# A LoRA router in four 32-column groups, copied and transposed back, and a later split of the next input

## The reference, cut to what matters

```python
def _mole(x, W, b, A, Bm, Rw):
    gates = jax.nn.softmax(jnp.einsum('bsd,de->bse', x, Rw), axis=-1)
    base = jnp.einsum('bsd,dh->bsh', x, W) + b
    z = jnp.einsum('bsd,edr->ebsr', x, A)
    zg = z * jnp.transpose(gates, (2, 0, 1))[..., None]
    lora = jnp.einsum('ebsr,erh->bsh', zg, Bm)
    return base + SCALING * lora
h = _mole(x, W1, b1, A1, B1, R1)
h = jax.nn.relu(h)
return _mole(h, W2, b2, A2, B2, R2)
...
h = _layernorm(x, axis=-1) * (1 + cb) + sb
x = x + gb * _L1_ffn_ref(h, ...)
```

## Time and profile before

| | |
|---|---|
| median of 3 runs | 516.0 us (515.77 to 517.62) |
| the profiled execution | 514.19 us, its span 512.3 us |
| busy, share of the span | PE 482.0 us (94%), DVE 349.8 us, ACT 340.1 us, POOL 170.4 us |
| LoRA turns 2 to 6, from one to the next | 10.9 us each |

### The profile page before, as it was taken

How to read it: one execution, slowest core, us unless ns; L and a number is a source line. 1 busy time by engine, 2 the same in 40 slices (tenths; PEclk the granted TensorE clock), 3 DMA queues, 4 the chain that set the end, 5 groups by cost and what they waited for, 6 DMA issues and landing times.

```text
span 512.3 us, 11888 instructions
## 1 busy us (share of the span) xinstructions
PE 482.0 (94%) x4560; PEld 387.1 (76%) x4560; DVE 349.8 (68%) x1009; ACT 340.1 (66%) x648; POOL 170.4 (33%) x244
## 2 busy tenths in 40 slices
PE   8699989999999999998997999999999998999994
PEld 6567877787678777876776777877877687998884
DVE  6986887779686978373685876778767673545433
ACT  4968958775877578965765676766767555555640
POOL 2610540034102201210426347274472815343311
PEclk9869999999999999999999999999999999999998
DMA  8600000000000300000322221312213000001001
GB/s 297 207 0 2 2 0 1 0 3 0 1 1 2 142 1 1 1 1 7 116 80 89 80 75 59 113 49 77 86 47 110 7 3 0 22 22 41 22 22 41
DMA packets 24250, 23.44 MB, mean 46 GB/s; under 512 B 3808, under 2 KB 22944, under 8 KB 24064
## 3 DMA queue, kind: packets, MB, share of 16 engines
q1 hardware_dynamic: 23136, 22.12, 13.9%
q10 hardware_dynamic: 1056, 0.52, 0.4%
HBM read 20.27 MB, written 2.36 MB: 44 GB/s over the span
## 4 chain that ended last, share of the span: by engine, by line
PE 43%; issue 3%; POOL 2%; DVE 1%; ACT 1%; SPq 1%; DMA 1%; POOLq 0%
PE bank L170 6%; PE bank L2098 6%; PE bank L172 5%; PE bank L171 5%; PE bank L2008 5%; PE bank L2059 3%; PE bank L2033 3%; PE bank L2048 3%; PE bank L2021 2%; PE bank L246 2%; PE bank L2075 1%; PE bank L2089 1%; PE bank L2068 1%; SPq L1752 1%; DMA att_prob<-cut_rows 1%
## 5 line engine op out<-in xcount | busy, mean ns | idle before, releaser
L1119 PE MATMUL bank<-ffn_g_hi,w_hi 128*128 128x512 f32 x288 | 116.9, 406 | 0.1
L1120 PE MATMUL bank<-ffn_g_lo,w_hi 128*128 128x512 f32 x288 | 114.0, 396 | 0.0
L654 DVE TENSOR_TENSOR ffn_g_lo<-ffn_full,ffn_g_hi 128x512 fp32r<-128x512 f32 x96 | 67.1, 699 | 27.3 <-ACT ffn_full L902 25.9
L1119 PEld LDWEIGHTS bank<-ffn_g_hi,w_hi 128*128 128x128 f32 x288 | 54.3, 188 | 14.0 <-issue 1.9
L1120 PEld LDWEIGHTS bank<-ffn_g_lo,w_hi 128*128 128x128 f32 x288 | 54.3, 188 | 11.7
L902 ACT ACTIVATE ffn_full<-bank,cols 128x512 f32<-128x512 f32 x64 | 44.2, 696 | 21.5 <-PE bank L1120 16.4
L1665 POOL TENSOR_TENSOR att_vw<-att_v,att_prob 128x128 f32<-128x128 f32 x64 | 25.0, 415 | 83.1 <-DVE att_prob L1477 83.1
L1854 ACT COPY att_qT<-bank 128x512 f32<-128x512 f32 x64 | 37.1, 589 | 12.4 <-PE bank L172 8.4
L1477 DVE TENSOR_TENSOR_SCAN att_prob<-att_prob,bank 128x512 f32<-128x512 f32 x32 | 37.5, 1206 | 6.8 <-DMA att_prob<-cut_rows 6.7
L1488 DVE TENSOR_TENSOR att_prob<-bank,att_prob 128x512 f32<-128x512 f32 x32 | 21.9, 690 | 23.6 <-PE bank L2008 22.6
L2098 PE MATMUL bank<-l,att_qT 128*128 128x155 f32 x256 | 37.4, 298 | 0.2 <-ACT att_qT L1827 0.2
(11 more groups left out here) (233 smaller groups left out, 1148.6 us busy)
## 6 DMA issues: line engine op xcount, KB each, us to landing
att_prob<-cut_rows SPq DMA_DIRECT2D x64, 128.0 KB, 3.0
att_wide<-cum_rows SPq DMA_DIRECT2D x64, 56.0 KB, 2.0
out<-att_vw SPq DMA_DIRECT2D x7, 256.0 KB, 2.3
x<-in_x SPq DMA_DIRECT2D x3, 512.0 KB, 11.7
w_raw<-in_w_all SPq DMA_DIRECT2D x1, 1152.0 KB, 8.5
w_raw<-in_w_all SPq DMA_DIRECT2D x1, 768.0 KB, 9.8
x<-in_x ACTq DMA_DIRECT2D x2, 256.0 KB, 3.4
w_raw<-in_w_all SPq DMA_DIRECT2D x1, 512.0 KB, 5.0
```

Of the source, the lines that this page charges most:

```text
L654: dve.tensor_tensor(lo, full[j % 4][:, :], hi.bitcast(F32), ALU.subtract).then_inc(low, 1)
L1119: pe.matmul(acc, w[0], x[0], start=start, stop=False)
L1120: return pe.matmul(acc, w[0], x[1], start=False, stop=stop)
```

## The change

Turns 1 to 6 compute the first router of the next sequence, so of sequences 2 to 7, in another way. The weight is now `ar1` padded with zeros to 32 columns, and the tokens stream: four matmuls of 128x128, one for each token tile, write four groups of 32 PSUM partitions of one bank (`down_rows`, through the helper that the attention gates use, L267 in both kernels). ACT copies that 128x128 block to SBUF (`keep_rows`), and one TensorE transpose puts the tokens back on the partitions (`down_turn`), in the layout that `route` reads. The transpose stands between the two halves of `layer2`, and `layer2_end` moves behind the second half. `bring_high` moves behind `keep_rows` and `ranks(b - 1, 1)`. The bank table follows: the rows take bank 1, the transposed result bank 0, behind the flip of the next input. The order of `layer2_end` and `layer2(b, 1)` changes in turn 7 too.

```diff
@@ constants and weights
-L_WAR2 = L_AR1 + AR
+L_WAR2 = L_AR1 + GLO
-        r["ar1"] = r["l1"][:, L_AR1:L_AR1 + AR]
+        r["ar1"] = r["l1"][:, L_AR1:L_AR1 + GLO]
@@ lora_uses, turn(b)
+                if more:
+                    uses.append((("rows", b + 1, 0), 1))
                 if back:
                     uses.append((("ranks", b - 1, 1), hid_home[b % 2]))
+                uses += ends(b)
                 if more:
-                    uses.append((("down", b + 1, 0), 1))
-                uses += ends(b)
+                    uses.insert(len(uses) - 1, (("down", b + 1, 0), 0))
@@ ACT
+                def keep_rows(b):
+                    act.wait_ge(ring_mm, full("rows", b, 0))
+                    act.copy(router_rows[b % 2][:, :], bank("rows", b, 0)[:, 0:P]).then_inc(rows_ready, 1)
@@ ACT, the turn
                         relu(b, m)
                         if more and m == 1:
                             bring_full(B + b + 1)
-                        if more and m == 2:
-                            bring_high(B + b + 1)
+                    if more:
+                        keep_rows(b + 1)
                     ranks(b - 1, 1)
                     if more:
+                        bring_high(B + b + 1)
                         exps(b + 1, 0)
@@ TensorE
+                def down_rows(b):
+                    pe.wait_ge(h_ready, B + b - 1)
+                    ps = claim(pe, "rows", b, 0)
+                    group_mm(pe, ps, r["ar1"], hT[b % 2]).then_inc(ring_mm, 1)
+                def down_turn(b):
+                    pe.wait_ge(rows_ready, b - 1)
+                    ps = claim(pe, "down", b, 0)
+                    pe.transpose(ps[:, 0:P], router_rows[b % 2][:, :], r["ident"][:, :]).then_inc(ring_mm, 1)
@@ TensorE, the turn
                     if b == 1:
                         output(LAST)
+                    if more:
+                        down_rows(b + 1)
                     flip_ranks(b - 1, 1)
+                    layer2(b, 0)
                     if more:
-                        down(b + 1)
-                    layer2(b, 0)
+                        down_turn(b + 1)
+                    layer2(b, 1)
                     layer2_end(b - 1)
-                    layer2(b, 1)
                     if more:
                         flip_ranks(b + 1, 0)
```

More of the change, by code:

```diff
@@ L261, in gate_rows, with group_mm @@
     return slice(t * GLO, t * GLO + NH)
-def gate_mm(pe, ps, r, hT):
+def group_mm(pe, ps, w, hT):
     for t in range(T):
-        mm = pe.matmul(ps[t * GLO:(t + 1) * GLO, 0:P], r["wg"][:, :], hT[:, t * P:(t + 1) * P], start=True, stop=True)
+        mm = pe.matmul(ps[t * GLO:(t + 1) * GLO, 0:P], w[:, :], hT[:, t * P:(t + 1) * P], start=True, stop=True)
     return mm
@@ L1213, in run @@
                                     pe.wait_ge(att_h_ready, 1)
-                                    gate_mm(pe, claim(pe, "alpha", 0), r, r["h_full"][0]).then_inc(mm, 1)
+                                    group_mm(pe, claim(pe, "alpha", 0), r["wg"], r["h_full"][0]).then_inc(mm, 1)
                         y(i, 0)
@@ L1325, in attention_lora @@
         lora_mm, hid_ready, scaled, res_ready, stored = sem("lora_mm"), sem("lora_hid_ready"), sem("lora_scaled"), sem("lora_res_ready"), pair_sems("stored")
-        end_ready = sem("lora_end_ready")
+        end_ready, rows_ready = sem("lora_end_ready"), sem("lora_rows_ready")
+        router_rows = [sb(f"lora_rows{s}", [P, P]) for s in slots]
         def step_uses(b):
@@ L1410, in __call__ @@
                         "cross": (outer_ready, 2 * b + k + 1), "y": (added, b + 1),
-                        "down": (zg_ready[0], b + 1), "ranks": (zT_ready[k % 2], b + 1), "hid": (hid_ready, b * KH + k + 1),
+                        "down": (zg_ready[0], b + 1), "rows": (rows_ready, b - 1), "ranks": (zT_ready[k % 2], b + 1), "hid": (hid_ready, b * KH + k + 1),
                         "e": (scaled, 2 * b + k + 1),
@@ L1971, in alpha @@
                     ps = claim(pe, "alpha", b, 0)
-                    gate_mm(pe, ps, r, hT[b % 2]).then_inc(ring_mm, 1)
+                    group_mm(pe, ps, r["wg"], hT[b % 2]).then_inc(ring_mm, 1)
                 def values(b):
@@ L2067, in down @@
                     for t in range(T):
-                        mm = pe.matmul(ps[:, t * 32:t * 32 + AR], hT[b % 2][:, t * P:(t + 1) * P], r["ar1"][:, :], start=True, stop=True)
+                        mm = pe.matmul(ps[:, t * 32:t * 32 + AR], hT[b % 2][:, t * P:(t + 1) * P], r["ar1"][:, 0:AR], start=True, stop=True)
                     mm.then_inc(ring_mm, 1)
+                def down_rows(b):
[6 more added lines that the diff above has]
+                    pe.transpose(ps[:, 0:P], router_rows[b % 2][:, :], r["ident"][:, :]).then_inc(ring_mm, 1)
                 def flip_ranks(b, k):
@@ L2236 @@
         "v_all": v_all, "B12": b12,
-        "l1": np.concatenate([tiles(a["L1_attn_Wo"], 2), A1, a["L1_ffn_R1"], tiles(WAR2, KH), bg], 1),
+        "l1": np.concatenate([tiles(a["L1_attn_Wo"], 2), A1, a["L1_ffn_R1"], np.zeros((D, GLO - AR), np.float32), tiles(WAR2, KH), bg], 1),
         "wg": wg,
```

## The result

The changed kernel takes 519.94 us at the median of 22 runs, the kernel before 517.11 at the median of its 22 taken beside it. The ratio is 1.0057, 95% interval 1.0041 to 1.0072: slower by 2.1 to 3.7 us. Runs of either kernel scatter over some 5 us, and much of that arises before the LoRA turns: in the twelve traces here DVE's addition in turn 1 starts anywhere from 431.4 to 436.2 us. So I compare the stretch that the change touches inside the traces. I measure it from the start of DVE's addition in turn 1 to the start of the last addition of all.

The account below looks back on a forecast made before the run. TensorE bounds turns 2 to 6, a DVE and ACT chain the end. Turn 1 +0.25 to +0.37, turns 2 to 5 0 to +0.48, turn 6 -0.10 to -0.24, end +2.17: near +2.6, so 518.6 us, range 516.9 to 520.3.

Parts of the forecast that it names:

- rival 2: Turns 1 to 5: a further wait, the first router's gating late by 0.3 us; +1.5, 520.1 us; chance 0.13.
- The router's cost on TensorE: Turns 2 to 6: new matmuls 0.46 to 0.56 us plus transpose replace 0.81, saving 0.10 to 0.24 a turn.
- The relay over ACT and POOL: Turns 2 to 5: high piece to ranks copy becomes the bound, turns 10.91 to 11.03 us; 0 to +0.48 in all.
- my zero: The place behind layer 1 on TensorE, 454.59 in the old trace, from which the relay's steps are counted.
- Turn 1: Rows wait for DVE's addition with the ranks' transposes now behind them, so L2088 comes +0.25 to +0.37 us later.
- Turn 6: No normalise in this turn, so TensorE's saving counts: -0.10 to -0.24 us.
- The order behind turn 7: layer2_end behind both halves of layer 2 delays scaling and the gatings behind it on DVE: +2.17 us, the largest term.
- The clock: Last stretch: all that follows scaling was taken to keep its length, with no clock term in the sum.
- The first router's gating: Starts later, behind the new transpose; 0.25 to 0.35 us left before the ranks' transposes, so costed at nothing.
- Rival 1: Relay over ACT and POOL does not bind, TensorE keeps its saving in turns 2 to 6; 517.0 to 517.7 us; chance 0.24.
- Rival 3: route_end(0) hangs on layer 2's second half, not scale(6), and the router saves 0.34 a turn; 514.3 us; chance 0.04.
- Rival 4: New router's column groups run one after another, 0.8 to 0.9 us and not 0.36; 520.6 us; chance 0.03.

Follow-up runs that it names:

- e4: Changed kernel with layer2_end ahead of layer 2's second half in turn 7 and POOL's rescale ahead of its low piece; ratio to the kernel before 0.9963.
- e9: Changed kernel with POOL's rescale ahead of its low piece and layer2_end ahead of layer 2's second half in every turn; ratio to the kernel before 0.9954.
- e3: Changed kernel with POOL's rescale ahead of its low piece, the high piece left as changed; ratio to the kernel before 1.0019.
- e1: Changed kernel with layer2_end ahead of layer 2's second half in turn 7 alone, as before; ratio to the kernel before 1.0022.
- e6: Changed kernel with 24 unused transposes of the identity on TensorE behind the last layer2_end; ratio to the kernel before 1.0062.
- e8: Changed kernel with DVE's scale(6) behind both route_end, TensorE's order untouched; ratio to the kernel before 1.0004.
- e7: Changed kernel with the new router's four matmuls all writing the same 32 partitions, one column group; a single run, 521.36 us.
- e2: Changed kernel with the high piece (bring_high) back behind the third relu, as before; ratio to the kernel before 1.0048.

## Why the prediction was right, point by point

I gave 518.6 us and a range of 516.9 to 520.3, on a median of 516.0. The median of the changed kernel is 519.94; that of the kernel before moved to 517.11 with more runs, so the difference is 2.83, where I had 2.6.

Part of that is luck. In the traces the stretch grew by 3.35, outside my sum of 2.2 to 2.9: the clock's 0.45 was not in it, and the relay cost 0.60 where my bound was 0.48. The profiled execution took 518.69, where I had 516.4 to 517.1. The range held the median because it was wide enough for rival 2, which did not come, and of the 1.34 us between 518.6 and 519.94, 1.11 are the rise of the median before. The interval of the difference, 2.1 to 3.7 us, holds the 2.83, the 3.35 and my 2.6 alike. The mechanism is what the traces bear out, term by term.

**The router's cost on TensorE.** The group was 0.35 us, its lead-in 0.11 (0.34 from the wide matmul ahead, in place of 0.23), and the transposes behind it took 0.48 for 0.45: 0.49 in all, inside my 0.46 to 0.56, and the new transpose 0.11. That is a saving of 0.21, inside my 0.10 to 0.24. But the turns of e4 show 0.32; I had named 0.34 as the far end, for another reason. What I did not see is the order of layer 2: its halves take 2.15 and 2.02 us to the next start, 4.17, with the single transpose between them, for 4.27 with the LoRA addition between (in e9, with the new router, 4.32). This error did not show, since the relay swallows the saving in turns 2 to 5.

**The relay over ACT and POOL.** Right in its place and its links: low piece, `rescale`, `normalise`, copy, L2107, and e3 shows that one swap takes it off. Counted from my zero, which in the changed turn 3 is 456.30 (0.23 behind the wide matmul at 456.07), low piece, `normalise`, copy and L2107 stand at 2.48, 5.75, 7.31 and 7.92, each inside its bounds. The turn was 11.07 and not 10.91 to 11.03. The term at fault is the last: from L2107 to my zero I took 3.06 from a turn in which L2088 does not wait, and it is 3.15. Behind the wait the start of L2107 to the next matmul is 0.34 (464.22 to 464.56), not 0.23. The copy of the ranks was also 0.68 behind its transposes' start, not 0.63, but that lay inside the bounds.

**Turn 1**: +0.33 for +0.25 to +0.37. **Turn 6**: -0.20 for -0.10 to -0.24, and this too by luck: TensorE saved its full 0.32, and 0.11 went back because the turn begins behind a wait at L2107 (10.70 of e1 and e6 for 10.59 of e4). **The order behind turn 7**: +2.13 for +2.17, and e1 and e8 show it to be that order, on DVE's side.

**The clock**: missed. I wrote that all that follows the scaling keeps its length. The steps on DVE and ACT do, those on TensorE do not, which stood idle for 2.94 us ahead of its last groups; +0.45, shown by e6.

**The first router's gating** ended at 461.82, its transposes began at 462.03 on TensorE's own account, so 0.2 us were left of the 0.25 to 0.35 that I gave; with a transpose and handover of 0.2 to 0.3 my own numbers give 0.2 to 0.35. **Rival 1** (the relay does not bind) is out by e3. **Rival 2** did not come. **Rival 3** fell on DVE's order, as argued; its condition, made true by moving `scale`, is e8. **Rival 4** is out by the 0.35 of the group and by e7.

On rival 4 the measurement and the Trainium skill part. The Trainium skill, "TensorE: Matmul & The Clock Gate", section "Part 3: Packing small matmuls", says that weight loads overlap matmuls in flight only where row groups differ; four groups that differ in columns alone took 0.35 us here, with their loads, and 0.99 in one group. The measurement decides. It agrees in kind with the same section's table, which has 2.38 times for three column groups at 512 columns; here it is 2.8 for four at 128. By the Trainium skill, "ScalarE: Activation LUTs", section "What ACT_TABLE_LOAD costs", my estimate for the new copy was 0.29 us; the trace has 0.26.

## What to carry to other kernels

When work is taken off the bounding engine, add up the longest relay over the other engines that comes back to it, and look for the link that waits out of program order only: here `rescale` needed nothing of the low piece that it stood behind. A saving on the bounding engine is worth no more than that relay's slack. At the end of a program the same edit meets another bound: ask of each moved step who stands behind its waiter there, and whether TensorE has more to do after a long idle time.

## What the runs showed of the hardware that I had not expected

- TensorE idle for 2.94 us, with matmuls at 2.4 GHz before, had its first two groups behind it at full speed (0.42 and 0.44 us) and the last two at 1.2 GHz (0.63 and 0.69). The point is not fixed: e7 and e3, with the same 2.94, had 0.66 and 0.54 for the third group and 0.69 for the last, and in e2 all four came at 1.2 GHz (0.66, 0.69, 0.66, 0.69). With 0.78 us of idle time at that place (e4) or 0.32 behind the filler (e6) the level held until the matmuls were through. What in the idle time decides it is not shown.
- The first wide matmul behind a wait is 0.34 us from the next, not 0.23. So is the first behind four transposes without a wait (454.33 to 454.67), and the last ahead of a group of narrow columns (456.07 to 456.41). A wait thus costs more than the timeline shows as idle: at L2107 it shows 0.20, but L2107 starts 0.60 behind the matmul before it (463.62 to 464.22) in place of 0.23, and loses another 0.11 behind it. That makes 0.48, the 11.07 of this turn less the 10.59 of e4.
- Four column groups of 32 side by side take 0.35 us, in one group 0.99: 2.8 times as long, for eight passes of 128 columns.
